# Conv taps read from PSUM, the product by D on ScalarE, and wider spacing behind the centring of a norm

## What is computed

```python
x = x + 0.5 * ffn(layernorm(x))          # 32 experts of 96, top 6, and a shared one of 192
h = layernorm(x);  r = rmsnorm(h)
z, xx, B, C, dt = split(r @ in_proj)     # z 512, xx 128 repeated to 512, B 128, C 512, dt 128
dt = softplus(dt @ dt_proj + b)
xx = silu(conv4(xx) + conv_b)            # causal, four taps along the tokens, per channel
state = exp(dt * A) * state + (dt * xx) * B;  y = sum(state * C)   # scan over 256 tokens, 16 states
h = h + ((y + xx * D) * silu(z)) @ out_proj
h = h + mlp(rmsnorm(h))                  # gated, inner width 1024
x = x + h
x = x + 0.5 * ffn(layernorm(x))
```

## Time and profile before

| | |
|---|---|
| median of three runs | 1793.18 us |
| lowest run | 1792.14 us |
| profiled execution, device time | 1797.3 us |
| profiled execution, span from first to last instruction | 1795.5 us |
| mean granted TensorE clock, share of full speed | 0.947 |
| busy share of the span | PE 87%, DVE 72%, POOL 55%, ACT 47% |

### The profile page before, as it was taken

One profiled execution on the slowest core, in us unless ns is written; L12 is line 12 of the kernel. 1 busy time (PEld: TensorE's weight loads), 2 busy tenths in 40 slices (PEclk: granted clock), 3 DMA queues, 4 the chain that ended last, 5 costly groups with the idle time before them and its releaser, 6 DMA issues. The chain is left out here.

```text
span 1795.5 us, 22504 instructions
## 1 busy us (share of the span) xinstructions
PE 1556.8 (87%) x7088; PEld 1136.3 (63%) x7088; DVE 1288.6 (72%) x2085; ACT 842.9 (47%) x1676; POOL 993.8 (55%) x1048
## 2 busy tenths in 40 slices
PE   6878888777788999899998999899985999868979
PEld 5756555655676666666666666666663666647868
DVE  4536995478968878687959887887857776679421
ACT  4434543545624563356534663456433553445323
POOL 2523676345545766376646666476633766348525
PEclk9989999978989999999999999999996999979989
DMA  6863223332332323242333223232321332224434
GB/s 220 318 206 98 78 82 101 96 100 85 101 105 90 115 84 110 70 138 78 111 102 118 83 90 112 85 129 84 105 79 41 123 100 102 82 86 158 145 104 147
DMA packets 72278, 200.25 MB, mean 112 GB/s; under 512 B 9921, under 2 KB 22433, under 8 KB 71777
## 3 DMA queue, kind: packets, MB, share of 16 engines
q1 hardware_dynamic: 63968, 173.65, 29.1%
q0 software_dynamic: 8192, 25.17, 4.8%
HBM read 173.62 MB, written 23.59 MB: 110 GB/s over the span
## 5 line engine op out<-in xcount | busy, mean ns | idle before, releaser
L737 PE MATMUL gub<-x_hi,wr 128*128 128x512 f32 (+1 forms) x1040 | 425.4, 409 | 50.6 <-DVE hid L1107 44.8
L1397 POOL TENSOR_TENSOR ring<-ring 128x512 f32<-128x512 f32 x192 | 253.6, 1321 | 307.4 <-DVE ring L1277 306.2
L1376 POOL TENSOR_TENSOR hid<-hid,u_sb 128x512 f32<-128x512 f32 (+1 forms) x260 | 289.6, 1114 | 236.1 <-ACT u_sb L970 199.0
L818 PE MATMUL acc<-hid,w_down 128*128 128x512 f32 (+1 forms) x1040 | 408.9, 519 | 1.8 <-POOL hid L1376 1.8
L739 PE MATMUL gub<-x_hi,wr 128*128 128x512 f32 (+1 forms) x1040 | 370.8, 357 | 0.0
L738 PE MATMUL gub<-x_lo,wr 128*128 128x512 f32 (+1 forms) x1040 | 370.2, 356 | 0.0
L1271 DVE TENSOR_TENSOR_SCAN ring<-decays,side 128x512 f32<-128x512 f32 x256 | 310.5, 1213 | 28.9 <-ACT decays L1069 24.6
L970 ACT ACTIVATE u_sb<-gub 128x512 f32<-128x512 f32 (+1 forms) x260 | 132.7, 510 | 347.3 <-PE gub L739 346.8
L980 ACT ACTIVATE hid<-gub 128x256 f32<-128x256 f32 (+1 forms) x324 | 156.8, 484 | 278.2 <-PE gub L739 153.7
L1384 POOL TENSOR_TENSOR hid<-hid,weight 128x512 f32<-128x512 f32 (+1 forms) x240 | 272.9, 1137 | 15.8
L737 PEld LDWEIGHTS gub<-x_hi,wr 128*128 128x128 f32 x1040 | 205.4, 197 | 93.6 <-issue 58.1
(11 more groups left out here) (120 smaller groups left out, 1823.3 us busy)
## 6 DMA issues: line engine op xcount, KB each, us to landing
wr<-w_halves SPq DMA_DIRECT2D x234, 512.0 KB, 3.3
wm_gu<-in_w_mlp POOLq DMA_DIRECT2D x64, 256.0 KB, 3.1
w_halves<-wr SPq DMA_DIRECT2D x26, 512.0 KB, 4.9
wm_down<-in_w_mlp POOLq DMA_DIRECT2D x64, 128.0 KB, 2.6
w_raw<-in_w_gu SPq DMA_DIRECT2D x26, 256.0 KB, 4.3
rows<-parts SPq DMA_DIRECT2D x16, 384.0 KB, 2.3
cst<-rows SPq DMA_DIRECT2D x48, 128.0 KB, 2.6
xin<-in_x SPq DMA_DIRECT2D x8, 256.0 KB, 2.9
```

The source lines that it names most:

```text
L737: mm(out, w[:, 0, half, k, :], x_hi[:, k, a:b], start=(k == 0), stop=False)
L818: last = mm(acc[k][:, a:b], w, h[:, a:b], start=(c == 0), stop=(c == (MLP_CHUNKS if mlp else FFN_CHUNKS) - 1))
L1376: nc.gpsimd.tensor_tensor(h, h, u_sb[c % USLOTS][:, a:b], ALU.mult).then_inc(sem["hidden"], 1)
L1397: add(ysum, ysum, ring[:, u % 3], ALU.add).then_inc(sem["y_sum"], 1)
```

## The change

- Item `x` on ACT and the tile `xpad` are gone. The taps read the projection where PE left it, in the side bank. The order of the taps is turned round: the tap of the token itself comes first and writes all 256 columns with the bias, and the later ones add to 255, 254 and 253 columns, so no padding is needed. The two items are now `xc` and `xd`, of four instructions each as before; the side bank is free after the last tap of `xd`, not after ACT's copy.
- Item `y0` is done by ACT (`Copy` with a per-partition scale), not by DVE. ACT waits there for `sp_x` of the same half.
- In a front, `xc` and `xd` stand right behind `x`, ahead of `dt` and `sl`.
- In `SPACE`, the lengths of `nc` (2 to 5), `nm` (2 to 4), `n1` of `rms1` (1.4 to 4) and `nm` of `rms1` (2 to 5) grow, and `x` shrinks (2 to 1.4).

```diff
-    return [("split", 0, when), ("sr", 0, when), ("x", 0, when), ("sl", 0, when), ("xc", 0, when, 0),
-            ("dt", 0, when), ("xc", 0, when, 1), ("xt", 0, when), ("sp", 0, when), ("xm", 0, when),
+    return [("split", 0, when), ("sr", 0, when), ("x", 0, when), ("xc", 0, when), ("xd", 0, when), ("sl", 0, when),
+            ("dt", 0, when), ("xt", 0, when), ("sp", 0, when), ("xm", 0, when), ("split", 1, when), ("sr", 1, when),
...
-ENDS = {"ub": "unit", "z": "zm", "split": "sr", "n1": "nc"}
+ENDS = {"x": "xd", "ub": "unit", "z": "zm", "split": "sr", "n1": "nc"}
...
-SPACE = {"n1": 1.4, "nc": 2, "n2": 3, "nm": 2, "rq": 0.75, "split": 1.4, "sr": 2, "sl": 2, "x": 2, "xc": 2, "xt": 2,
+SPACE = {"n1": 1.4, "nc": 5, "n2": 3, "nm": 4, ("n1", "rms1"): 4, ("nm", "rms1"): 5, "rq": 0.75, "split": 1.4, "sr": 2, "sl": 2, "x": 1.4, "xc": 2, "xd": 2, "xt": 2,
...
-             "z": [("z_done", 1)], "x": [("x_padded", 1)],
+             "z": [("z_done", 1)], "x": [("conv", TAPS)],
...
+                elif kind == "y0":
+                    act.wait_ge(sem["dtx"], s.count("dtx", ("sp_x",) + it[1:], 1))
+                    for j in range(2 * it[1], 2 * it[1] + 2):
+                        A(y[:, j, :], xs[:, j, :], ACT.Copy, scale=vecs[:, j, 0:1]).then_inc(sem["y_init"], 1)
...
-                elif kind == "x":
-                    act.wait_ge(sem["side_filled"], s.count("side_filled", it, 1))
-                    if (least := s.count("conv", it, 0)) is not None:
-                        act.wait_ge(sem["conv"], least)
-                    A(xpad[:, :, TAPS - 1:], pair(s.side_of(it)), ACT.Copy).then_inc(sem["x_padded"], 1)
...
-                            o, i = xs[:, j, :], xpad[:, h, k:k + SEQ]
+                            j, late = 2 * it[1] + h, TAPS - 1 - k
+                            o, i = xs[:, j, late:SEQ], pair(s.side_of(of))[:, h, 0:SEQ - late]
...
-                elif kind == "y0":
-                    dve.wait_ge(sem["dtx"], s.count("dtx", ("sp_x",) + it[1:], 1))
-                    for j in range(2 * it[1], 2 * it[1] + 2):
-                        v.tensor_scalar(y[:, j, :], xs[:, j, :], vecs[:, j, 0:1], None,
-                                        ALU.mult).then_inc(sem["y_init"], 1)
```

More of the change, by code:

```diff
@@ L97 @@
     "zm": {"z_done": 1},
-    "x": {"side_filled": 1, "x_padded": 1},
+    "x": {"side_filled": 1},
     "xc": {"conv": TAPS},
+    "xd": {"conv": TAPS},
     "xt": {"x_tanh": 1},
@@ L196, in emit @@
             return
+        if it[0] == "xd":
+            emit(("xc",) + it[1:])
         fills = it[0] in FILLS and kind_of(it) != "n1r"
@@ L266, in items_of @@
         assert at(("shift",)) < at(("n1", "lnA")) and at(("ub", UNITS // 2)) < at(("split", 0, "next"))
-        assert at(("yz", 1)) < min(at(("xc", 0, "next", 0)), at(("z", 0, "next")))
+        assert at(("yz", 1)) < min(at(("xc", 0, "next")), at(("z", 0, "next")))
     if ln2:
@@ L395 @@
 }
-ENDED_BY = {"g": "by_g", "ub": "unit", "z": "zm", "split": "sr", "n1": "nc"}
+ENDED_BY = {"x": "xd", "g": "by_g", "ub": "unit", "z": "zm", "split": "sr", "n1": "nc"}
 BANKS = {"side": SIDES, "gub": GUBS}
@@ L1012, in do @@
                       scale=0.5).then_inc(sem["z_tanh"], 1)
[L1013 to L1017 removed]
                 elif kind == "xt":
[L1019 removed]
+                    act.wait_ge(sem["conv"], s.count("conv", ("xd",) + it[1:], TAPS))
                     if (least := s.count("part_lo", it, 0)) is not None:
@@ L1083, in _ @@
                 v.memset(decay[i][:, :, 0:1], 0.0).then_inc(zeroed, 1)
[L1084 to L1085 removed]
+            dve.wait_ge(zeroed, 5)
             dve.wait_ge(a_exp, 1)
@@ L1190, in do @@
                                            ALU.add, ALU.mult).then_inc(sem["z_done"], 1)
-                elif kind == "xc":
-                    dve.wait_ge(sem["x_padded"], s.count("x_padded", ("x",) + it[1:3], 1))
+                elif kind in ("xc", "xd"):
+                    of = ("x",) + it[1:]
+                    dve.wait_ge(sem["side_filled"], s.count("side_filled", of, 1))
+                    if kind == "xd":
+                        dve.wait_ge(sem["conv"], s.count("conv", ("xc",) + it[1:], TAPS))
+                    taps = range(TAPS - 1, TAPS // 2 - 1, -1) if kind == "xc" else range(TAPS // 2 - 1, -1, -1)
+                    done = 0
                     if (least := s.count("y_gated", it, 0)) is not None:
                         dve.wait_ge(sem["y_gated"], least)
-                    for k in range(TAPS // 2 * it[3], TAPS // 2 * (it[3] + 1)):
+                    for k in taps:
                         for h in range(2):
-                            j = 2 * it[1] + h
-                            o, i = xs[:, j, :], xpad[:, h, k:k + SEQ]
+                            j, late = 2 * it[1] + h, TAPS - 1 - k
+                            o, i = xs[:, j, late:SEQ], pair(s.side_of(of))[:, h, 0:SEQ - late]
                             w = vecs[:, j, 3 + k:4 + k]
-                            if k == 0:
+                            if late == 0:
                                 v.tensor_scalar(o, i, w, vecs[:, j, 2:3], ALU.mult,
@@ L1203, in do @@
                             else:
-                                done = 2 * (k - TAPS // 2 * it[3]) + h - 1
-                                dve.wait_ge(sem["conv"], s.count("conv", it, done))
+                                if done > 1:
+                                    dve.wait_ge(sem["conv"], s.count("conv", it, done - 1))
                                 v.scalar_tensor_tensor(o, i, w, o, ALU.mult,
                                                        ALU.add).then_inc(sem["conv"], 1)
+                            done += 1
                 elif kind == "xm":
```

21 lines of the change are left out of this document (8 added, 13 removed).

## The result

The changed kernel took 1810.9 us, the kernel before 1793.1 beside it: a ratio of 1.0101 (95% interval 1.0081 to 1.0121), 18 us slower. That is within 2%, but on the other side of no change than the forecast of 1771, and outside its range.

The account below looks back on a forecast made before the run. PE was taken to bound the kernel, DVE a stretch of turn 2. 7.2 + 2.1 + 2.9 + 12.0 + 4.0 = 28.2, less 6.4: 21.8 us off 1797.3, 1775.5; that execution lay 4.1 above the median, so 1771 us, range 1748 to 1790.

Parts of the forecast that it names:

- The taps' price: On DVE, all 128 taps priced at 0.416 us from PSUM, first taps included: 53.2 us, 27.0 less.
- The product: Product by D leaves DVE (29.4 us); ACT gains 16 us, loses copies of 9.6: +6, hidden unless ACT waits for `sp_x`.
- Turn 2: DVE sets the time from 371 to 436 us: taps and products there save 7.2 us, the norms' spacing 2.1.
- Where the savings land: DVE sheds 56 us; counted: turn 2 7.2 and 2.1, turn 1 2.9, steady turns 12.0, turns 7 and 8 4.0.
- the taps of one half come a unit earlier: In a steady turn's MLP stage, earlier taps, each pair somewhat cheaper, were counted as 1.0 us won.
- The rival of the clock: Enough waits shrink that PE's clock stays up, in turns 2 to 8: 22 us more won, 1749 us; chance 0.16.
- The bank: Bank of `x` held until the eighth tap; PE's wait taken as 0.4 us for each of 16 halves, 6.4 us lost.
- the rival of the bank: PE waits the whole eight taps in each half, 16 x 3.3 = 53 us against 28.2: 1818 us; chance 0.06.
- The spacing: At `lnA` and `rms1`, more room before PE's second matmul shortens the square's wait: 2.1 us in turn 2, 1.2 per steady turn.
- without that cover, a chunk's wait of some 1 us per turn: Later items move closer, `ln2` routing about a chunk later; lighter DVE was to cover this, else some 1 us per turn.

Follow-up runs that it names:

- y0_alone: The kernel before with nothing but the product by D moved to ACT: 1787.4 us, 0.9971 of the kernel before.
- spacing_back: The changed kernel with the old spacing numbers for the norms, all other edits kept: 1786.6 us, 0.9967 of the kernel before.
- bank_freed_back: The changed kernel with the old spacing and x copied out of its bank by ACT, the shortened taps reading the copy: 1764.1 us, 0.9839 of the kernel before.
- n2_behind: The changed kernel with n2 of ln1 moved from ahead of ub 11 to behind it in turns 1 to 5: 1800.8 us, 1.0043 of the kernel before.
- front_order: The kernel before with the front's new order and its shorter spacing of x; padded copy, taps and product as before: 1782.0 us, 0.9926.
- front_order_y0: The kernel before with the front's new order, its spacing of x, and the product by D on ACT: 1766.1 us, 0.9841.

## Why the prediction was wrong

**The taps' price: right in kind.** 53.2 us forecast, 56.0 measured, none stretched. The first tap was undersized: 539 ns, not 416. From its median of 408 ns in the kernel before, 32 x (539 - 408) ns is 4.2 us. By the page cited in the prediction ("VectorE: DVE Perf Modes" of the Trainium skill, section "Why PSUM operands drop a tier") the estimate was 4 us lost for these 32. The trace now agrees with the page. The prediction set it aside because 401 ns looked like the single rate.

**The product: right in sum, not in place.** It cost ACT 14.4 us in place of the copies' 9.6, and ACT waited 4.3 us for `sp_x` in all. Alone it brought 5 us; the prediction's 3.0 in turn 2 and 0.8 in each steady turn make 6.2. But in the trace of y0_alone turn 2 is no shorter (213.9 against 213.7 us), while the steady turns gain 0.3 to 2.4.

**Turn 2: the largest term of the sum did not come.** 9.3 us were forecast there, 7.2 of them because "a microsecond taken off it is a microsecond won". DVE's busy time in turn 2 fell by 8.3 us in the changed kernel (162.9 to 154.6), and the turn by 2.0. In y0_alone it fell by 3.9 and the turn grew by 0.2; in spacing_back it fell by 7.2 and the turn by 1.2; only in bank_freed_back did the turn follow, by 5.6 for 5.5. So what is taken off DVE there is not won by itself; what else sets the turn was not followed.

**Where the savings land: 28.2 us without bank and spacing, 28 to 29 measured, but not from the terms summed.** Part of that sum was the cheaper taps; with taps that cost what they cost before, the gain is the same. A step that failed here is the one that gave the new order of the front only 1.0 us in a steady turn ("the taps of one half come a unit earlier") and put no price on `dt` going behind the taps. That order takes 12 us out of the MLP stages of turns 3 to 8, with 4.5 in turn 4, there nearly all by the clock. The rival of the clock named this mechanism (more won than the waits themselves), but hung it on the waits and not on the order. That the sum came out is chance.

**The bank: a wait sized far too small.** "I take 0.4 for each of 16 halves, 6.4 us", since `near()` puts `xd` ahead of any item that would need the bank. Measured: 37 us, less 14 for the cheaper taps. The bound from above, 3.3 us a half, was the right size of a wait; it stands in nine places, 3.1 us each, as the rival of the bank had it for all sixteen. Not seen was that it falls into the MLP stages, which get 2.7 to 5.4 us longer by it. The row taken for the price (waits of 0.4 us for a bank's last reader) shows waits behind a single short instruction, not behind eight taps with a gate and a unit's product (L1263) among them.

**The spacing: wrong sign.** -2.1 in turn 2 and -1.2 in each steady turn were forecast; +24 us measured. In the steady turns the square's wait did go, but it goes with the old spacing as well. The price "I count nothing; without that cover, a chunk's wait of some 1 us per turn" is the step that failed. The list of items was read at the norms that get more room (`lnA`, `rms1` in turn 2) and not at `ln1`, which shares the numbers. There one place decides whether 3.5 us of ACT stand ahead of a unit's decays or behind them. Of all the steps this one is furthest from what was measured: a gain of 6.9 us in the sum, a cost of 24.

**Not settled.** The swap explains ten of the spacing's 24 us, the numbers of `lnA` and `rms1` another 8. In the expert stages of turns 3 to 5, 5.2 to 5.3 us longer in the changed kernel than in spacing_back, the two are the whole: 2.6 to 2.9 us each. The 5 or 6 us that remain belong to `ln1` and `ln2`. Turn 1 is of that size: it is still 6 us longer in n2_behind than in spacing_back, and neither `lnA` nor `rms1` stands in it. In the changed kernel much of turn 1's loss is the clock, 0.92 against 0.95 before:

```profile
111.40:318.50 207.10, 176.81 (x673) 114.37 (x671) 138.62 (x205) 94.35 (x179) 112.75 (x98) 0.92 0.29 95
```

PE is busy 5.9 us longer there with the same 673 matmuls (170.88 us before); what makes the clock fall there is not shown.

## What to carry to other kernels

When a table of lengths sets an order, follow every item that shares the number that is changed, and look for the one that changes sides with something that an engine in order is awaited for; the item that the number was meant for may be the smaller part. When a buffer's reader becomes slower or later, price the hold as a whole wait at the use that needs it next, in the stage where that use stands, with what the clock does after the wait. And test order apart from price: the new order of the front, for which the prediction counted 1.0 us in a steady turn, gained 13 us alone and 28 with the product.

## What the runs showed that was not expected

The stretch did not go away with the taps. Taps and product took 24 + 29 = 53.6 us off DVE, but DVE's busy time fell by 42.8. Other instructions that read and write SBUF alone got longer, with the same work: the product of a norm by its weight, and the gate `yg`. Before, then after:

```profile
L1282 DVE TENSOR_TENSOR yg<-xs,z 128x256 f32<-128x256 f32 x32 | 26.5, 827 | 4.5 <-POOL xs L1403 4.5
...
L1172 DVE SCALAR_TENSOR_TENSOR rn<-hn_next,lnw,rstd 128x256 f32<-128x256 f32 x16 | 9.0, 604 | 2.8 <-ACT rstd L998 2.8
```

```profile
L1283 DVE TENSOR_TENSOR yg<-xs,z 128x256 f32<-128x256 f32 x32 | 31.1, 971 | 7.7 <-POOL xs L1404 7.6
...
L1171 DVE SCALAR_TENSOR_TENSOR rn<-hn_next,lnw,rstd 128x256 f32<-128x256 f32 x16 | 13.9, 911 | 10.5 <-ACT rstd L999 10.5
```

What makes them longer was not tested.

And the sum of PE's waits does not tell the clock. In turn 4's MLP stage the granted clock was 0.88 before, with waits of 3.4, 2.4 and 1.3 us, and 0.88 with spacing_back (3.3, 3.2 and two short ones). It was 1.00 with front_order, front_order_y0 and bank_freed_back (3.2, two that make 2.5, and 1.2 or 1.3), at nearly the sum of before. The stage then took 36.5 or 36.6 us instead of 41.1 and 41.9. But the list of the waits does not tell it either: in front_order the MLP stages of turns 3, 4 and 5 have the same waits (3.2, two that make 2.5, 1.3), and the clock was 0.91, 1.00 and 0.95, the time 39.4, 36.6 and 37.5 us. What decides is not shown.
